# Where the first pair's adapter input is split, where small loads are issued, and who issues the last store

## The reference, cut to what matters

```python
attn_out = softmax((x @ Wq) @ (x @ Wk).T * scale) @ (x @ Wv) @ Wp + bp
cms_out  = gelu(attn_out @ cW1 + cb1) @ cW2 + cb2 + one_hot(code)
modifier = gelu(concat([attn_out, cms_out]) @ mW1 + mb1) @ mW2 + mb2
y0       = clip(x + cms_out + modifier, 0, 1)
```

```python
h = gelu(y @ W_down[e] + b_down[e]) @ W_up[e] + b_up[e]   # 512 -> 256 -> 512
y = layernorm(y + h) * gamma[e] + beta[e]
```

## Time and profile before

| | us |
|---|---|
| timed runs: median (lowest, highest) | 1188.05 (1183.38, 1188.11) |
| profiled execution, whole | 1184.63 |
| its span in the trace | 1182.8 |
| PE (matmul) busy | 1166.8, 99% of the span |
| DVE, ACT, POOL busy | 763.2, 531.4, 162.4 |
| granted TensorE clock | full, mean 0.999 |
| DMA, mean over the span | 212 GB/s |

### The profile page before, as it was taken

One profiled execution on the slowest core, in us unless ns is written; L12 is line 12 of the kernel. 1 busy time (PEld: TensorE's weight loads), 2 busy tenths in 40 slices (PEclk: granted clock), 3 DMA queues, 4 the chain that ended last, 5 costly groups with the idle time before them and its releaser, 6 DMA issues.

```text
span 1182.8 us, 15571 instructions
## 1 busy us (share of the span) xinstructions
PE 1166.8 (99%) x5276; PEld 965.3 (82%) x5276; DVE 763.2 (65%) x1352; ACT 531.4 (45%) x965; POOL 162.4 (14%) x146
## 2 busy tenths in 40 slices
PE   9999999999999999999999999999999999999997
PEld 7888888878888788888888888888888878788886
DVE  6344386776767866666567576775464636788786
ACT  5434354564544534343435535533131303347887
POOL 1332130000000000000000000000000000349981
PEclk9999999999999999999999999999999999999999
DMA  5754453546654727263699688656767678936644
GB/s 206 274 203 164 178 178 124 170 142 223 215 167 163 274 92 257 96 243 108 248 399 321 231 295 309 216 172 193 230 191 230 195 211 283 350 143 217 222 167 196
DMA packets 113014, 251.25 MB, mean 212 GB/s; under 512 B 13333, under 2 KB 13333, under 8 KB 109607
## 3 DMA queue, kind: packets, MB, share of 16 engines
q1 hardware_dynamic: 112934, 250.25, 61.9%
HBM read 154.78 MB, written 95.43 MB: 212 GB/s over the span
## 4 chain that ended last, share of the span: by engine, by line
PE 89%; DVE 4%; DMA 3%; ACT 2%; issue 1%; POOL 1%; SPq 0%; ACTq 0%; DVEq 0%
PE psum L742 85%; DMA prep<-wdu_dram 2%; PE psum L1011 2%; DMA ring<-up_operands 1%; POOL prep L1952 1%; PE psum L795 1%; DVE c_op L1618 1%; DMA res<-y_spill 1%; PE psum L949 0%; ACT prep L1051 0%; PE psum L791 0%; PE psum L803 0%; ACT res L1355 0%; DVE ring L1508 0%; PE psum L776 0%
## 5 line engine op out<-in xcount | busy, mean ns | idle before, releaser
L742 PE MATMUL psum<-a_op,ring 128*128 128x512 f32 x1344 | 316.8, 389 | 2.8 <-DMA ring<-up_operands 2.5
L742 PEld LDWEIGHTS psum<-a_op,ring 128*128 128x128 f32 x1344 | 252.0, 188 | 56.1 <-issue 2.9
L742 PE MATMUL psum<-g_hl,w_hl 128*128 128x512 f32 x1152 | 263.7, 389 | 0.4 <-DVE w_hl L1569 0.4
L742 PEld LDWEIGHTS psum<-g_hl,w_hl 128*128 128x128 f32 x1152 | 216.1, 188 | 46.1 <-DVE w_hl L1569 0.8
L742 PE MATMUL psum<-c_op,ring 128*128 128x512 f32 x672 | 163.3, 390 | 0.4 <-DVE c_op L1618 0.3
L742 PEld LDWEIGHTS psum<-c_op,ring 128*128 128x128 f32 x672 | 125.8, 188 | 27.8 <-DVE c_op L1618 1.8
L1167 ACT ACTIVATE g<-g,sm 128x512 f32<-128x512 f32 x96 | 69.5, 724 | 137.4 <-DVE g L1556 66.7
L1576 DVE TENSOR_TENSOR g_hl<-g,g_hl 128x512 fp32r<-128x512 f32 x96 | 66.1, 689 | 52.0 <-ACT g_hl L1190 51.2
L1147 ACT CAST ring<-asum 128x256 fp32r<-128x256 f32 x96 | 38.5, 404 | 104.0 <-PE psum L742 76.1
L1190 ACT CAST g_hl<-g 128x512 fp32r<-128x512 f32 x96 | 58.5, 618 | 53.4 <-PE psum L742 53.4
L1958 POOL MEMSET acc_u<- 128x1024 f32 x1 | 1.0, 954 | 592.3 <-DVE w_hl L1569 592.3
(11 more groups left out here) (154 smaller groups left out, 1590.4 us busy)
## 6 DMA issues: line engine op xcount, KB each, us to landing
up_operands<-ring SPq DMA_DIRECT2D x168, 256.0 KB, 2.9
ring<-up_operands SPq DMA_DIRECT2D x168, 256.0 KB, 3.0
wdu_split<-prep SPq DMA_DIRECT2D x36, 512.0 KB, 2.9
down_operands<-stage SPq DMA_DIRECT2D x56, 256.0 KB, 4.7
ring<-down_operands SPq DMA_DIRECT2D x56, 256.0 KB, 2.9
rawp<-up_w_dram SPq DMA_DIRECT2D x24, 512.0 KB, 4.8
wraw<-dn_w_dram SPq DMA_DIRECT2D x48, 256.0 KB, 3.9
wd<-wdu_split SPq DMA_DIRECT2D x12, 1024.0 KB, 8.7
```

The costliest lines, as they stand in the source:

```text
L742: ins = nc.tensor.matmul(ps, lw(el), rw(er), start=first and i == 0, stop=last and i == 2, skip_group_check=skip)
```

## The change

1. The parts of the first pair's y0 are neither made in chunks 10 and 11 nor stored nor loaded. Once `res[:, 0]` and `res[:, 1]` have landed, ACT makes the high parts from them (`y0_hi(0)`, `y0_hi(1)`, ahead of its first `h_gelu`), DVE the low part of sequence 0 (after its last `down_product_add`, ahead of `y0_rows(0)`), POOL the low part of sequence 1. Two waits of chunk 12 on the removed stores go, or become the wait on the y0 stores.
2. The four `bup0` loads are issued three ring loads apart. `wd[0]` and `wd[1]` are loaded in halves (512 KB) after ring loads 5, 7 and 15, 17, and `wu[0]` (1 MB) after ring load 11, counted by `at_` (ring load number less the number of the last quad's first step, less 6).
3. In the last row block of G the two cross passes are taken bank by bank instead of pass by pass, and PE waits for both low parts first.
4. The last store of the result is issued by ACT instead of SP.

```diff
...
@@ -436,6 +431,8 @@
         DOWN = QC
+
+        WD_AT, WU_AT = ((5, 7), (15, 17)), 11
         Y0_ADD_AT = 2, 3, 5, 6
@@ -587,13 +584,6 @@
-            def y0_split_piece(k):
-
-                b, h, e = k // 4, k // 2 % 2, k % 2
-                part = slice(2 * h, 2 * h + 2)
-                sp.wait_ge(y0_lo_done, 2 * b + h + 1)
-                sp.dma_start(y0_split[b, :, e, part, :], xs[:, b, part, :] if e else f(y0_h[:, b, part, :])).then_inc(s_y0split, 16)
-
@@ -618,33 +608,31 @@
                 if ci == NCHUNK + 3:
-                    for k in range(4, 8):
-                        y0_split_piece(k)
                     continue
...
                         y0_piece(k - 1)
-                    if ci == NCHUNK + 2 and k > 0:
-                        y0_split_piece(k - 1)
                 down_weights(4 * ci + 4)
...
-            def split_rows(b, k):
-
-                e, part = k // 2, slice(k % 2 * 2, k % 2 * 2 + 2)
-                sp.wait_ge(aop_used, aop_at(NCH - 1, 1) + LAYER_STEPS[1].index((P5, 0)) + 1)
-                sp.wait_ge(s_y0split, 16 * 8)
-                sp.dma_start(f(yT[b][:, e, part, :]), y0_split[b, :, e, part, :]).then_inc(s_yTin[b], 16)
-
             split_sets = wdu_split.rearrange("(s c) p e n -> s c p e n", c=NPC)
+
+            def unit_down_part(u, e):
+
+                sp.dma_start(f(wd[u % 2][:, e, :, :].rearrange("p (c k) n -> p c (k n)", c=DT * KB // PC)),
+                             split_sets[bass.ds(u // B * EXPERTS + ex[u % B], 1), 0:DT * KB // PC, :, e, :].rearrange("o c p n -> p (o c) n")).then_inc(t_wd[u % 2], 16)
...
                     sp.wait_ge(t_down, (u - 1) * MT)
+                if u < 2:
+                    for e in range(2):
+                        unit_down_part(u, e)
+                    return
                 sp.dma_start(f(wd[u % 2][:, :, :, :].rearrange("p e (c k) n -> p e c (k n)", c=DT * KB // PC)),
@@ -680,28 +668,23 @@
                     x_late_in((r - PREPARED) // COPS - 1)
-                if r == PREPARED + 3 * COPS + 2:
+                bup_at = r - PREPARED - 3 * COPS - 2
+                if bup_at % 3 == 0 and 0 <= bup_at < 3 * B:
+                    b = bup_at // 3
                     sp.wait_ge(x_added, 2)
-                    for b in range(B):
-                        sp.dma_start(bup0[:, b, :], bup_all[bass.ds(ex[b], 1)].to_broadcast([P, V])).then_inc(t_bup0, 16)
+                    sp.dma_start(bup0[:, b, :], bup_all[bass.ds(ex[b], 1)].to_broadcast([P, V])).then_inc(t_bup0, 16)
                 at_ = r - last_up - RING
-                if at_ in (3, 6, 9, 12):
-                    split_rows(0, at_ // 3 - 1)
-                if at_ == 15:
-                    unit_down(0)
-                if at_ == 19:
-                    split_rows(1, 0)
-            split_rows(1, 1)
+                for u in range(2):
+                    if at_ in WD_AT[u]:
+                        unit_down_part(u, WD_AT[u].index(at_))
+                if at_ == WU_AT:
+                    unit_up(0)
             sp.wait_ge(s_spill, 16 * 4)
...
             sp.dma_start(res[:, 0, :, :], y0_dram[:, 0]).then_inc(s_y0in[0], 16)
-            for k in (2, 3):
-                split_rows(1, k)
             sp.wait_ge(aop_used, dop_at(NCH - 1, 11) + 1)
...
             sp.dma_start(res[:, 1, :, :], y0_dram[:, 1]).then_inc(s_y0in[1], 16)
-            unit_down(1)
-            unit_up(0)
             unit_up(1)
@@ -728,8 +711,6 @@
                 sp.dma_start(out[3, :, i, :], res[:, 3, i, :]).then_inc(s_out, 16)
-            sp.wait_ge(t_yf, 11 * DT + 4)
-            sp.dma_start(out[3, :, 1, :], res[:, 3, 1, :]).then_inc(s_out, 16)
             sp.wait_ge(s_out, 16 * 8)
@@ -789,13 +770,17 @@
                         nc.tensor.matmul(bank[HIGH + m], wqT[:, 0, k, m * P:(m + 1) * P], wkT[:, 0, k, :], start=k == 0, stop=False)
-                    for el, er in ((1, 0), (0, 1)):
-                        pe.wait_ge(qk_split, 2 * k + er + 1)
+                    if k < DT - 1:
+                        for el, er in ((1, 0), (0, 1)):
+                            pe.wait_ge(qk_split, 2 * k + er + 1)
+                            for m in range(DT):
+                                nc.tensor.matmul(bank[HIGH + m], wqT[:, el, k, m * P:(m + 1) * P], wkT[:, er, k, :], start=False, stop=False)
+                    else:
+                        pe.wait_ge(qk_split, 2 * k + 2)
                         for m in range(DT):
-                            ins = nc.tensor.matmul(bank[HIGH + m], wqT[:, el, k, m * P:(m + 1) * P], wkT[:, er, k, :],
-                                                   start=False, stop=k == DT - 1 and er == 1)
-                            if k == DT - 1 and er == 1:
-                                ins.then_inc(bank_full, 1)
+                            for el, er in ((1, 0), (0, 1)):
+                                ins = nc.tensor.matmul(bank[HIGH + m], wqT[:, el, k, m * P:(m + 1) * P], wkT[:, er, k, :], start=False, stop=er == 1)
+                            ins.then_inc(bank_full, 1)
@@ -951,7 +936,7 @@
             def t_down_mm(u, b):
-                pe.wait_ge(t_wd[u % 2], 16 * (u // 2 + 1))
+                pe.wait_ge(t_wd[u % 2], 16 * (u // 2 + 2))
                 for m in range(MT):
@@ -961,10 +946,10 @@
                     for k in range(DT):
-                        if m == 0 and u < 2:
-                            pe.wait_ge(s_yTin[u], 64)
+                        if m == 0 and u == 0:
+                            pe.wait_ge(t_y0lo0, k + 1)
                         elif m == 0 and u < B:
-                            pe.wait_ge(t_y0lo, (u - 2) * DT + (k + 1))
+                            pe.wait_ge(t_y0lo, (u - 1) * DT + (k + 1))
                         elif m == 0:
@@ -1197,7 +1182,6 @@
                         act.wait_ge(s_spill, 16 * 4)
-                        act.wait_ge(s_y0split, 16 * 8)
                 if i in (P6, P7, P5, P4):
@@ -1246,10 +1230,6 @@
                                              bias=cbias[:, 2 * p + seq, m:m + 1]).then_inc(d_evac, 1)
-
-            def first_pair_y0_hi(seq, h):
-                act.wait_ge(y0_done, 2 * seq + h + 1)
-                nc.scalar.copy(y0_h[:, seq, 2 * h:2 * h + 2, :], xs[:, seq, 2 * h:2 * h + 2, :]).then_inc(y0_hi_done, 1)
@@ -1302,8 +1282,6 @@
                         second_pair_hi(SECOND_PAIR_HI[DOWN, d])
-                    if ci in (NCHUNK + 2, NCHUNK + 3) and d < 2:
-                        first_pair_y0_hi(ci - NCHUNK - 2, d)
                 if ci % NCHUNK == 4 - 1:
@@ -1311,7 +1289,10 @@
                 for d in range(DT):
-                    act.wait_ge(y0_done, DT * (b - 1) + d + 1)
+                    if b < 2:
+                        act.wait_ge(s_y0in[b], 16)
+                    else:
+                        act.wait_ge(y0_done, DT * (b - 1) + d + 1)
                     nc.scalar.copy(yT[b][:, 0, d, :], res[:, b, d, :]).then_inc(t_y0hi, 1)
@@ -1355,6 +1336,8 @@
+            y0_hi(0)
+            y0_hi(1)
             for s in range(14):
@@ -1375,6 +1358,8 @@
             y_scale(11)
+            act.wait_ge(t_yf, 11 * DT + 4)
+            nc.scalar.dma_start(out[3, :, 1, :], res[:, 3, 1, :]).then_inc(s_out, 16)
@@ -1597,7 +1582,7 @@
                     else:
-                        dve.wait_ge(s_y0split, 16 * 8)
+                        dve.wait_ge(s_spill, 16 * 4)
                         for k in range(STG):
@@ -1628,13 +1613,6 @@
                 nc.vector.tensor_scalar(part, part, 0.0, 1.0, ALU.max, ALU.min).then_inc(y0_done, 1)
-
-            def first_pair_y0_lo(seq, h):
-
-                dve.wait_ge(y0_hi_done, 2 * seq + h + 1)
-                dve.wait_ge(s_spill, 16 * 2 * (seq + 1))
-                part = xs[:, seq, 2 * h:2 * h + 2, :]
-                nc.vector.tensor_tensor(part, part, f(y0_h[:, seq, 2 * h:2 * h + 2, :]), ALU.subtract).then_inc(y0_lo_done, 1)
@@ -1790,8 +1768,6 @@
                         y0_clip(*divmod(d, 2))
-                    if ci in (NCHUNK + 2, NCHUNK + 3) and 1 <= d <= 2:
-                        first_pair_y0_lo(ci - NCHUNK - 2, d - 1)
                 if ci % NCHUNK == 4 - 1:
@@ -1804,10 +1780,9 @@
-                if b >= 2:
-                    dve.wait_ge(t_y0lo, (b - 1) * DT)
                 dve.wait_ge(t_rows_full, (b + 1) * DT)
                 for i in range(DT):
+                    dve.wait_ge(*((t_y0lo, (b - 1) * DT + i + 1) if b else (t_y0lo0, i + 1)))
                     nc.vector.tensor_tensor(res[:, b, i, :], UP[i], bup0[:, b, :], ALU.add).then_inc(t_res_done, 1)
@@ -1909,6 +1884,9 @@
             down_product_add(NCH - 1, 6)
+            for d in range(DT):
+                dve.wait_ge(t_y0hi, d + 1)
+                nc.vector.tensor_tensor(yT[0][:, 1, d, :], res[:, 0, d, :], f(yT[0][:, 0, d, :]), ALU.subtract).then_inc(t_y0lo0, 1)
             y0_rows(0)
@@ -1957,9 +1935,9 @@
-            for b in range(2, B):
+            for b in range(1, B):
                 for d in range(DT):
```

(5 more changed lines are left out.)

## The result

The change made the kernel slightly slower. Twenty runs of each gave 1190.14 us after (1187.39 to 1193.22) and 1187.07 us before (1183.38 to 1190.91), a ratio of 1.0025 with a 95% interval of 1.0016 to 1.0034. The profiled execution took 1188.91 us, its span 1187.0, against 1184.63 and 1182.8. The forecast was 1183.0.

A forecast was written before the change was run, and what follows sets the result against it. PE was taken as the bound, busy 1166.8 of 1182.8 us; 2.50 + 0.65 - 0.1 + 0 = 3.05 us off 1184.63 gives 1181.6, off 1188.05 gives 1185.0. Forecast between: 1183.0, own range 1180.5 to 1186, 8-in-10 range 1178.5 to 1188.5.

The forecast's parts named there:

- The bias rows: PE's wait for a ring load until 959.91: spreading the four loads wins the whole 2.50 us; bounds 0 and 2.50.
- rival (a): Executions vary by PE's waits for ring loads behind long transfers, which the change thins; 0.5 to 0.7% faster; chance 0.26.
- The weight loads: Ring loads behind halved `wd` and `wu[0]`: the 0.96 us wait at 1006.02 goes, one up to 0.4 may come.
- rival (b): Spread rows and halved weights still delay ring loads: gain only 0.5 to 1.8 us; chance 0.14, shared with another rival.
- Where their gain goes: Before down(0): PE's 0.96 + 1.23 us become a wait of about 2.2 for DVE, costing +0.1; bounds -2.2, +1.3.
- What is queued behind: DVE's work before up(0): clips, `h_lo(0)`, `y0_rows(1)` move at most about 1.6 us, with three microseconds of room.
- ACT and POOL: Sequence 1's parts before down(1): `res[:, 1]` lands after 5.0 us, POOL's fourth slice at 1026.1, room 0.6, cost 0.
- Rival (c): Slower: `res[:, 1]` lands late and POOL's chain makes PE wait; 1187.0 from the profiled execution, 1190.4 from the median; chance 0.08.
- The first product: Last row block of G: bank-by-bank order lets PE go on 0.65 us sooner than 19.10; bounds 0 and 0.81.
- The last store: End of the kernel: issuing from ACT gains 0, as the DMA engines are 0.99 busy; bounds -0.1 to +0.5.
- The sum: Whole kernel: 2.50 + 0.65 - 0.1 + 0 = 3.05 us gained.

The follow-up runs named there:

- k5: The kernel before plus four idle POOL subtractions into a dead buffer beside DVE's rows and clips; one execution of 1184.36 us, not timed.
- k2: The changed kernel with items 2 to 4 undone, so only the split of y0 from its reload is new; 1193.86 us, 1.0061 to before.
- k11: The kernel before with only the bias row loads issued three steps apart; 1180.81 us, ratio 0.9958 to before.
- k3: The changed kernel with sequence 1's low part made by DVE instead of POOL, ahead of the clips; 1183.42 us, ratio 0.9974 to before.
- k4: k3 plus eight idle matmuls on PE ahead of down(0), filling its wait; 1182.15 us, ratio 0.9969 to before.
- k6: k3 with sequence 0's low part made ahead of DVE's last `down_product_add` instead of behind it; 1180.55 us, ratio 0.9963 to before.
- k9: The changed kernel with the eight clips on views taking every second element; 1189.52 us, ratio 1.0038 to before.
- k1: The kernel before with bias rows spread, bank-by-bank first product and last store by ACT; 1181.09 us, ratio 0.9962 to before.
- k7: k1 with `wd[0]` loaded in two halves instead of 1 MB at once; 1180.85 us, ratio 0.9967 to before.
- k8: k7 with sequence 1 alone split from its reload by ACT and DVE, sequence 0 keeping stored parts; 1179.31 us, 0.9957 to before.
- k10: k8 with `wd[1]` issued right behind the load of `res[:, 0]`; 1179.58 us, ratio 0.9952 to before.

## Why the prediction was wrong

Point by point, by its own steps.

**The bias rows: right, and worth more than the profiled execution showed.** The wait is gone. The four rows now land after 3.7 to 4.1 us and the ring loads behind them after 3.5 to 4.0 (4.9 expected). The 2.50 was one execution's price. k5 keeps the burst and shows 2.52 and a full clock; k2 keeps it too, and in its profile PE waits 3.34 us, the clock drops (0.73 over 955 to 965), and the 30 matmuls behind the wait take 9.9 instead of some 7.0 us, in all about 6.2. So the 4.1 us of k11 fit a stall that differs from run to run. The other runs of before fit it as well: in the three sessions the 12 with a mean granted clock of 0.996 or less have a median of 1187.1 us, the 20 with 0.998 or more 1184.3. That is the mechanism of rival (a), which was given 0.26; its time did not come, as the loss elsewhere was larger.

**The weight loads: right in this execution, not in every one.** The halves of `wd[0]` landed after 5.0 and 5.6 us, the ring loads behind them after 4.8 and 5.4 (4.3 to 5.5 and at most 6.6 expected). The one behind `wu[0]` took 6.9 (4.8 to 7.2), a wait of 0.2 (up to 0.4). k3 has the same loads, and there the load behind `wu[0]` took 7.8 us, more than the worst case, and PE waited 1.07 us at 997.07; k4, k6 and k9 have no such wait above 0.2. That is the mechanism of rival (b), in one execution of five, and behind the 1 MB that was left whole.

**Where their gain goes: right in the wait, wrong in its price.** PE waits 2.13 us before down(0) for DVE's subtraction; 2.2 was the forecast, by the same reasoning about DVE's order, and k6 shows that order to be the cause. But the step ended there. It had no term for the clock, and the 24 matmuls behind the wait took 1.56 us more; k4 shows that filling the gap removes exactly this. The stretch that "costs +0.1 us" should have been about +1.7.

**What is queued behind: this step failed.** It said that "the clips, `h_lo(0)` and `y0_rows(1)` move by about 1.6 us at most", with "three microseconds of room". It counted the starts of DVE's work and took the durations over from the trace of before. The change moved POOL's first subtraction from 1025.49 to 1017.13, on top of the clips. Eight clips took 10.39 instead of 2.76 us and the two `h_lo` 3.42 where before has 1.29 and k3, with POOL away from them, 1.28. Before, DVE stood for 1.5 us ahead of them:

```profile
1024.40 1.29 DVE L1821 TENSOR_TENSOR h_hl<-hf,h_hl 128x512 fp32r<-128x512 f32 x2 [1.47 <-ACT h_hl L1337]
```

So the chain of DVE began 2.9 us sooner (1017.26 against 1020.17), took 7.6 + 2.1 us more and lost 1.5 of standing, and the first bank of `y0_rows(1)` was done 5.3 us later (1031.59 against 1026.29). PE came to it 2.4 us sooner than before and had had 3.9 us in hand: 5.3 + 2.4 - 3.9 = 3.8, and 3.93 us of wait were measured, plus 2.64 of clock behind it. k3 takes this away and the ratio falls by 0.005; k5 makes the same clips long without any of the change. The evidence lay in the trace of before: one `h_lo` of 1.87 us beside POOL, where the others take 0.69 (the rows above).

The Trainium skill has this as a rule. Its page "SBUF — State Buffer", section "Who interferes with whom", says that GpSimd's SBUF ports are the second pair of VectorE's, and that whoever issues first gets that pair for the whole instruction while the other waits; VectorE needs it in a 2-port mode, which a `tensor_scalar` can enter, or with two inputs in SBUF beside a GpSimd instruction that reads SBUF. The trace agrees: `h_lo` (two inputs in SBUF) goes from 0.68 to 1.75 us, `y0_rows` (one input in PSUM) stays at 0.68, and the clip (one input in SBUF) goes from 0.416 to 1.51. That the clip runs in a 2-port mode no run shows; it shows that it is quicker than a two-input operation. Of the size the trace says somewhat less than strict turns: back to back and alone, POOL's subtractions start 1.25 us apart and clips 0.34, together 1.59, and a pair of them side by side takes 1.43.

**ACT and POOL: right.** `res[:, 1]` landed after 5.2 us (5.0 expected), POOL's first four subtractions were done at 1022.7, and down(1) started at 1022.07 with no wait. Rival (c) gave the right sign and a price like the true one (1187.0 from the profiled execution; 1188.91 came), but its mechanism, a late `res[:, 1]` with POOL's chain on PE's path, did not happen. POOL did not make PE wait for POOL; it made DVE late. That its price came near is chance.

**The first product: right.** Here the changed kernel's head:

```profile
17.21 2.06 ACT L1021 CAST g_w<-psum 128x512 fp32r<-128x512 f32 x4 [4.14 <-PE psum L782]
...
18.67 1.61 PE L723 MATMUL psum<-xT,g_w 128*128 128x512 f32 x6
```

PE goes on at 18.67, 0.43 sooner than in the earlier trace rows (0.65 expected), but the eight cross matmuls before it started 0.25 later, at 16.56; from there on it is 0.68 us less, as worked out. In the nine traces with this item the product starts at 17.5 to 18.7 us, in the four without it at 19.1 to 19.8. Later PE is further ahead: its product that starts at 392.22 us before starts at 390.71. Most of that comes between 63 and 94 us, where the same 130 matmuls take 30.5 us before and 29.5 after; but k2, without the item, has 29.5 there and k9, with it, 30.4, so this part differs between executions and can't be put down to the item. In the medians none of it can be seen: k1, which has it, and k11, which has not, lie 0.3 us apart in different sessions.

**The last store: it gained nothing, and here the end got longer.** From ACT's last group of results to the end are 1187.0 - 1179.21 = 7.8 us, and 7.4 before, 0.4 more where the bound was 0.1. k3, k4, k6 and k9, made from the changed kernel, have 7.8 as well; k1, k7, k8 and k10, which have the same store on ACT, have 7.4. So the issuer is not what costs it, and what does was not followed up.

**The sum, mended.** -3.05, then +1.56 and +2.64 for the clock and +3.93 for the clips' delay give +5.1 us; the profiled executions differ by 4.3, their spans by 4.2. The start is 1.51 ahead instead of 0.65 (-0.9), and the end 0.4 longer, which gives +4.6. The last 0.3 to 0.4 is not assigned.

## What to carry to other kernels

When a step moves to another engine, list what runs beside it at its new time, not only who waits for it: VectorE work on SBUF and GpSimd work should not share a stretch on the critical path, and here each VectorE operation without an input in PSUM was 1.1 us longer for it. A PE wait can have two prices, the wait and the matmuls behind it at half the clock (2.13 us of wait cost 3.7 here and 3.93 cost 6.6, but 1.22 and the 2.50 of the earlier trace rows no more than themselves), and in k4 and k6 filler and a reordering took the second away. Small broadcast loads in a burst before a tightly timed ring are worth spreading; here that edit alone gave, within the intervals, as much as the best of the other kernels.

## What the runs showed of the hardware

- POOL's two-input subtraction and DVE's operations on SBUF lengthen each other (before, after, k3, k5): clip 0.416 to 1.51 us, DVE's two-input subtraction 0.68 to 1.75, POOL's own 1.30 to 1.47 beside clips and 1.71 beside two-input subtractions. DVE operations with an input in PSUM stayed at 0.68 us beside POOL, and POOL's beside them at 1.30 (k5).
- A clip over every second float32 element took 0.421 us (k9), one over a whole row 0.416 (before).
- The waits of PE and the granted clock at their end and behind them: 1.22 us (k6), and 0.67 behind filler (k4), left it at 2.4 GHz; 1.93 (k3), 2.13 (after), 2.44 (k2), 3.34 (k2), 3.93 (after) and 3.95 (k2) came with 1.2 GHz for a part of the next 24 to 30 matmuls, 1.6 to 2.9 us lost by each. The 2.50 us of the earlier trace rows and the 2.52 of k5 did not. What PE had done just before differs: the waits of 1.93, 2.13 and 2.44 came right behind the 16 transposes of `y0_to_rows` (1.9 us), those of 2.50 and 2.52 right behind a product. Whether that is what decides was not tried.
